# Loading and normalising the first image in two halves, and rounding the first weights in two parts

## What is computed

```python
def _gn(v, G=32, eps=1e-05):
    g = v.reshape(B_, G, C_ // G, H_, W_)
    m, s = mean(g, axis=(2, 3, 4)), var(g, axis=(2, 3, 4))
    return ((g - m) / jnp.sqrt(s + eps)).reshape(v.shape)
x = basic_block(x, e0b0c1, e0b0c2)       # relu(conv3(relu(conv3(x, w1) * S), w2) * S + x)
x = basic_block(x, e0b1c1, e0b1c2); f0 = x
x = basic_block(x, e1b0c1, e1b0c2, stride=2, ds=e1b0ds)
x = basic_block(x, e1b1c1, e1b1c2); f1 = x
x = basic_block(x, e2b0c1, e2b0c2, stride=2, ds=e2b0ds)
x = basic_block(x, e2b1c1, e2b1c2)
x = (relu(deconv2(x, dec0w) * S) + f1) * S
x = (relu(deconv2(x, dec1w) * S) + f0) * S
```

## Time and profile before

| | us |
|---|---|
| median of 3 runs | 92.66 |
| lowest and highest run | 92.26, 92.81 |
| the profiled execution | 92.77 |
| its span, first to last instruction | 91.0 |
| PE busy in the span | 83.7 (92%) |
| DVE, ACT, POOL busy | 64.0, 44.7, 27.6 |

### The profile page before, as it was taken

One profiled execution on the slowest core, in us unless ns is written; L12 is line 12 of the kernel. 1 busy time (PEld: TensorE's weight loads), 2 busy tenths in 40 slices (PEclk: granted clock), 3 DMA queues, 4 the chain that ended last, 5 costly groups with the idle time before them and its releaser, 6 DMA issues.

```text
span 91.0 us, 1549 instructions
## 1 busy us (share of the span) xinstructions
PE 83.7 (92%) x537; PEld 74.2 (82%) x537; DVE 64.0 (70%) x190; ACT 44.7 (49%) x94; POOL 27.6 (30%) x43
## 2 busy tenths in 40 slices
PE   5998999999999999999999999999999989998700
PEld 3666999998777799999977777999999989886500
DVE  5559999799968799646625479999458797333820
ACT  6005214778445065744423359999900199962300
POOL 7300060999920000654440000300892004200330
PEclk9999999999999999999999999999999999999995
DMA  2888820034573013550000000000000000000094
GB/s 24 252 232 307 270 96 0 0 117 105 167 205 131 6 28 102 180 152 6 0 0 0 0 4 0 0 0 0 0 7 0 4 0 0 7 0 0 14 326 122
DMA packets 4183, 6.51 MB, mean 72 GB/s; under 512 B 464, under 2 KB 2000, under 8 KB 4176
## 3 DMA queue, kind: packets, MB, share of 16 engines
q1 hardware_dynamic: 4176, 6.42, 23.4%
HBM read 5.37 MB, written 1.05 MB: 71 GB/s over the span
## 4 chain that ended last, share of the span: by engine, by line
PE 82%; DVE 6%; DMA 4%; issue 1%; SPq 1%; ACT 1%; POOLq 1%
PE psum L828 76%; DMA x_sb<-x_in 4%; PE psum L867 2%; DVE split L724 1%; SPq L416 1%; PE psum L853 1%; PE psum L963 1%; POOLq L165 1%; PE psum L1020 1%; DVE shared L679 1%; DVE split L731 1%; DVE stats L608 1%; DVE moments L623 1%; DVE shared L637 1%; PE psum L860 1%
## 5 line engine op out<-in xcount | busy, mean ns | idle before, releaser
L469 POOL TENSOR_TENSOR odd<-relu,odd 128x363 fp32r<-128x363 f32 x12 | 13.4, 1135 | 16.0 <-ACT odd L544 16.0
L828 PE MATMUL psum<-shared,w_e0b0c 128*128 128x364 f32 x72 | 12.5, 331 | 0.4 <-DVE shared L637 0.4
L828 PEld LDWEIGHTS psum<-shared,w_e0b0c 128*128 128x128 f32 x72 | 12.0, 188 | 0.7 <-issue 0.7
L828 PE MATMUL psum<-shared,w_e0b1c 128*128 128x364 f32 x72 | 12.2, 329 | 0.0
L828 PEld LDWEIGHTS psum<-shared,w_e0b1c 128*128 128x128 f32 x72 | 12.1, 188 | 0.1
L828 PE MATMUL psum<-odd,w_e0b0c 128*128 128x512 f32 x48 | 12.0, 411 | 0.0
L828 PE MATMUL psum<-odd,w_e0b1c 128*128 128x512 f32 x48 | 12.0, 411 | 0.0
L754 DVE SCALAR_TENSOR_TENSOR relu<-psum,inside 128x363 f32<-128x363 f32 (+2 forms) x18 | 8.7, 489 | 3.8 <-PE psum L828 3.6
L828 PEld LDWEIGHTS psum<-odd,w_e0b1c 128*128 128x128 f32 x48 | 9.1, 190 | 2.6
L828 PEld LDWEIGHTS psum<-odd,w_e0b0c 128*128 128x128 f32 x48 | 9.1, 190 | 2.6
L544 ACT ACTIVATE odd<-relu 128x363 fp32r<-128x363 f32 x12 | 6.2, 518 | 7.4 <-DVE relu L754 7.4
(11 more groups left out here) (125 smaller groups left out, 139.0 us busy)
## 6 DMA issues: line engine op xcount, KB each, us to landing
out<-result SPq DMA_DIRECT2D x3, 256.0 KB, 3.1
x_sb<-x_in SPq DMA_DIRECT2D x4, 160.0 KB, 4.3
raw<-e0b0c_in SPq DMA_DIRECT2D x2, 256.0 KB, 4.9
raw<-e0b1c_in SPq DMA_DIRECT2D x2, 256.0 KB, 5.3
raw<-e1b1c_in SPq DMA_DIRECT2D x2, 256.0 KB, 3.0
raw<-e2b1c_in SPq DMA_DIRECT2D x2, 256.0 KB, 2.6
raw<-e1b0c_in SPq DMA_DIRECT2D x1, 448.0 KB, 3.7
raw<-e2b0c_in SPq DMA_DIRECT2D x1, 448.0 KB, 4.0
```

The lines of the kernel that those rows point to most:

```text
L469: pool.tensor_tensor(split_of(piece, 1), fp32_of(piece), split_of(piece, 0).bitcast(F32), ALU.subtract).then_inc(lo_ready, 1)
L828: last = pe.matmul(target, w, moving, start=(first and n == 0), stop=(final and n == len(terms) - 1), skip_group_check=skip)
```

## The change

Each image is loaded in two DMAs of 16 rows in place of three of 10, 12 and 10 rows, with two statistics instructions of 16 rows (512 values) for three. The vector of statistics is 12 numbers per partition in place of 18, and the spread one, which the matmul and L623 read, 48 in place of 72. ACT rounds the first weights in two instructions of two blocks each, with a signal of its own (w_hi_first) for the first. TensorE waits for that before the first two products of piece 0 and for w_hi before the other two, in place of w_hi before all. DVE waits for w_hi_first as well as w_hi before L642.

```diff
-STATS_ROWS = [(0, 10), (10, 12), (22, 10)]
+STATS_ROWS = [(0, 16), (16, 16)]
 VALUES = STATS * len(STATS_ROWS)
...
                 if image == 0:
-                    weights_hi(0)
+                    act.wait_ge(w_loaded[0], 16)
+                    for shift, signal in [(0, w_hi_first), (2, w_hi)]:
+                        act.activation(w_sb[0][:, 0, shift:shift + 2], raw[:, 0, shift:shift + 2, :],
+                                       ACT.Copy).then_inc(signal, 1)
                     act.wait_ge(zeros_set, 1)
...
                 if image == 0:
+                    dve.wait_ge(w_hi_first, 1)
                     dve.wait_ge(w_hi, 1)
...
-                pe.wait_ge(w_hi, k + 1)
+                if piece.index > 0:
+                    pe.wait_ge(w_hi, k + 1)
...
                 wait_source(piece, 0)
-                products(target, [(w[:, 0, s], moving(0, s)) for s in range(shifts ** 2)],
-                         first=not started, final=False)
+                high_terms = [(w[:, 0, s], moving(0, s)) for s in range(shifts ** 2)]
+                if piece.index == 0:
+                    pe.wait_ge(w_hi_first, 1)
+                    products(target, high_terms[0:2], final=False)
+                    pe.wait_ge(w_hi, 1)
+                    products(target, high_terms[2:4], first=False, final=False)
+                else:
+                    products(target, high_terms, first=not started, final=False)
```

More of the change, by code:

```diff
@@ L237, in build @@
         norm_lo = sem("norm_lo")
+        w_hi_first = sem("w_hi_first")
         w_hi = sem("w_hi")
```

## The result

The changed kernel takes 92.81 us (median of 20 executions, 92.43 to 94.25) against 92.43 for the kernel before (20 executions, 92.26 to 92.81). The ratio is 1.0035, 95% interval 1.0019 to 1.0052, or 0.32 us (0.18 to 0.48). The forecast was 92.40, faster. The time is inside the range and inside one per cent, but on the other side.

The account below looks back on a forecast made before the run. The chain to TensorE's first product at 8.58 us was taken as the bound. Landing -0.26, statistics +0.17, spread -0.02, sum -0.04, L623 -0.11 gave -0.26 us: 92.51 for the profiled execution, median 92.40; range 92.0 to 92.95.

Parts of the forecast that it names:

- What bounds the kernel: Whole kernel: one chain of waits to TensorE's first product at 8.58 us; an earlier start there moves the end equally.
- The landing of the second half: Load of image 0: second half lands at 4.90 us in place of 5.16, -0.26, bounds -0.45 and 0.
- The sign of being wrong that I had named: Image 0's statistics: the prediction is wrong if the second statistics instruction, L608, starts behind 5.3 us.
- Both reasons for an earlier landing: Load of image 0: 2048-byte rows may move at 369 GB/s against 286, and 0.47 us of SP's third issue is gone.
- The statistics: DVE, last piece of image 0: 512 values in place of 320 take 0.66 us, +0.17, bounds +0.16 and +0.23.
- Spread, sum, L623: Behind image 0's statistics: a third fewer values give -0.02, -0.04 and -0.11 us.
- Weights in two parts, waits at nothing: ACT's rounding and the added waits: second part ends 0 to 0.2 us later, covered, so 0 each.
- Rival 3: Load of image 0: larger second half lands at 5.67, 0.51 later; time 93.17 us; chance 0.10.
- Rival 2: Load of image 0: bytes alone set the landing, still 5.16; time 92.66 us; chance 0.17.
- Rival 4: TensorE's sum: clock rises no earlier, so an earlier sum runs slow and loses up to 0.14; 92.54 us; chance 0.09.
- Rival 1: TensorE before the sum: x lands so early that zero products hold the sum; gain 0.41, 92.25 us; chance 0.12.
- Rival 5: First weights: landing later than 7.5 makes w_hi last, early signal worth up to 0.3; about 92.5 us; chance 0.06.

Follow-up runs that it names:

- x_halves_only: Kernel before with only image 0's and the other images' loads and statistics in halves, weights rounded in one instruction: ratio 1.0033 to before, median 92.82 us.
- halves_19_zeros: Changed kernel with 19 zero products ahead of the sum in place of 22: ratio 1.0011 to the kernel before.
- changed_again: The changed kernel itself, unchanged, run once more for one execution: 92.50 us.
- halves_25_zeros: Changed kernel with 25 zero products ahead of the sum in place of 22: ratio 1.0041 to the kernel before.
- weights_split_only: Kernel before with only the weights rounded in two parts with their waits, three loads and statistics kept: 0.9982, median 92.39 us; measured again 1.0002, 92.38.
- halves_two_slots: Changed kernel with two 256-byte transfers behind the second half, so later loads are issued 0.94 us later: 1.0018 to before, median 92.61 us.
- small_last_one_slot: Kernel before with pieces of 14, 12 and 6 rows, weights in two parts, one 256-byte transfer behind the third piece: ratio 1.0026 to before.
- three_loads_19_zeros: Kernel before with weights in two parts and 19 zero products ahead of the sum in place of 22: ratio 0.9999 to before.
- third_load_by_act: Kernel before with weights in two parts, 19 zero products for 22, image 0's third piece issued by ScalarE at its start: 1.0045 to before.

## Why the prediction was wrong, step by step

**What bounds the kernel: right.** The first product moved by 0.29 us, the profiled execution by 0.30 (92.77 to 93.07), and TensorE's row behind it kept 59.59.

**The landing of the second half: wrong, and the step that turned the sign.** I put -0.26 (-0.45 to 0) on it. The sign of being wrong that I had named, a second L608 behind 5.3, came true: that instruction (L612 now) starts at 5.64. In the two first profiles the term was +0.45, and over five profiles against five +0.25 (means 5.22 and 4.97, with an uncertainty of about 0.13 on the difference). That the landing is what the time follows is plain from the five executions with halves issued by SP and no slot:

| kernel | landing | time | difference |
|---|---|---|---|
| the changed kernel | 5.61 | 93.07 | 87.46 |
| x_halves_only | 5.32 | 92.79 | 87.47 |
| halves_19_zeros | 5.18 | 92.65 | 87.47 |
| changed_again | 5.02 | 92.50 | 87.48 |
| halves_25_zeros | 4.98 | 92.46 | 87.48 |

With 87.47 behind it, the median of 92.75 (of the 18) stands for a landing at 5.28. Both reasons for an earlier landing failed. The pace of 369 GB/s did not come with the 2048-byte rows: with them the same stretch moved 225 GB/s, and the one from 2.5 to 5.5 us 262, against 245 before. And the removed issue was counted as a gain twice, for x and for what follows ("they are issued 0.47 earlier, so I count no wait"), when for x it was the cost. With the later loads held at their old place, or 0.47 behind it, the halves landed at 4.6 to 4.8, which is 0.3 to 0.6 ahead of the 5.16 that I started from: the direction of the forecast would have been right for that kernel, and its 4.90 a little late. What is shown so far is the landing. That the time comes back with it is not: these two kernels measured 1.0020 and 1.0018, between the changed kernel and the one before, with other waits in the landing's place.

**The statistics: sized 0.03 short.** Forecast 0.66, measured 0.69, so +0.20 in place of +0.17 against the 0.49 of before. The line that the Trainium skill, "VectorE: DVE Perf Modes", gives in the section on the trn2 errata, 151 cycles plus one per value at 0.96 GHz, has 0.69 and was the better estimate; the trace agrees with it.

**Spread, sum, L623: right.** Forecast -0.02, -0.04 and -0.11; measured -0.02 (0.22 for 0.24), -0.02 (0.42 against the 0.44 of weights_split_only, where the clock had risen before the sum as here) and -0.10 (0.38 for 0.48). With the statistics that makes +0.06 at equal landing. The profiles bear it out: weights_split_only has 92.39 - 4.98 = 87.41, the halves 87.47. The kernel before has 92.77 - 5.16 = 87.61, which is the same 87.41 and the 0.20 of its slow sum. So without any change of the landing the halves lose 0.06, and with the +0.25 of the profiles' means they lose 0.31, against 0.32 measured. That the two agree so closely is luck, given the 0.13 on the means. The 0.20 that the sum gained against the earlier trace rows in the first pair (0.62 to 0.42) was the clock and no part of the change.

**Weights in two parts, waits at nothing: right.** L529 took 0.71 for both parts against 0.61, inside the 0 to 0.2 that I gave, and ended at 8.41, before L641 at 8.76. ACT did not release the first product.

**The rivals.** Rival 3 is what happened in direction (slower, a landing behind 5.16), at 0.10, and its price was high, +0.51 for +0.32. Its cause, the size of the half, is refuted; what moves the landing is the loads issued behind it. Rival 2, an unchanged landing and so an unchanged time, is excluded by the interval of the ratio (0.18 to 0.48 us slower). Rival 4, a clock that rises too late for the sum, did not occur in the changed kernel's profile, whose sum took 0.42; it is in the profile of before, at 0.20. Rival 1 exists: it is the chain of halves_two_slots, but with a late clock on top (the sum took 0.63 at 6.00), and so without its gain. Rival 5, with the raw weights landing at 8.20 and ACT releasing the first product, exists in small_last_one_slot, but the low half of the weights took the gain. I had ended the landing's bounds at 0 in the forecast although the loss was one of my own cases, and I gave 0.58 to cases that gain from the landing on the strength of one profiled execution.

## What to carry to other kernels

Taking an issue out of a DMA queue also moves everything behind it forward, into competition with the load that is waited for; price a load by what is in flight beside it, and hold later loads back only as far as their own users allow (here `same_channel` and the first weights were next, within 0.5 us). A landing needs several profiles before it is a term of a sum: one kernel's varied by 0.6 us between executions, twice the effect that was forecast. And fewer, larger pieces lengthen the one operation that stands behind the last landing, which an average of busy time does not show.

## What was not expected of the hardware

The moment at which TensorE's clock rises is not fixed. The zero products come every 0.21 us at 1.2 GHz and every 0.12 or less at 2.4 GHz. In the profiles here the 22 of them took from 3.85 to 4.88 us from the same start at 1.07, so the rise came at different moments, and the sum took 0.41 to 0.44 when it came before and up to 0.71 when it came after. In two kernels with 19 zero products the 14 behind the sum ran at the slow pace as well, here in three_loads_19_zeros (profiled execution 93.73, timeline of PE):

```profile
1.08 4.24 PE L865 MATMUL psum<-zeros 128*128 128x256 bf16 x19 [1.08 <-DVE eps L662]
5.75 0.71 PE L858 MATMUL psum<-result,same_channel 128*128 128x72 f32 x2 [0.44 <-DVE result L615]
6.25 2.98 PE L865 MATMUL psum<-zeros 128*128 128x256 bf16 x13
```

The view ends at 9.0 and has 13 of them; all 14 take 3.19 us (in the timeline to 9.6) in place of 1.69 and end behind L641, so that the products of the first convolution start late, and the execution is 1.3 us longer. TensorE had been at work since 1.08 but idle for 0.44 before the sum. An idle stretch alone does not do it: third_load_by_act stood idle for 1.40 us before the sum, but its zero products had turned fast before that, and the 14 behind the sum took 1.69. In the two kernels with the slow 14, all 19 products ahead of the sum were slow. Among the 48 executions of the four kernels with 19 zero products 13 lie at 93.5 or above; among the 20 of the kernel before, whose profile has no idle stretch there, none does; among the 20 of the changed kernel, with its idle 1.0 us, two do, and one of the 12 of x_halves_only (94.29). That an idle stretch before the sum lets the rise slip where it has not come yet is argued from these counts and two profiles, and not shown: the kernel meant to show it, halves_25_zeros, had too few executions. The granted-clock column reads 1.00 in all these stretches and does not show the slow pace; the pace of the products does.
